# New instruction orders on TensorE, ScalarE and VectorE in a graph-attention stage, and its late weight preparation on GpSimd

## Chip, cores and metric

The kernel runs on one NeuronCore of one Trainium2 chip. The metric is the device time of one execution in microseconds (us); lower is better. It is measured three times for the kernel before, and once more under the profiler.

## What is computed

Two layers run one after the other on x (16 graphs, 512 nodes, 128 features). The first, the graph layer, is the stage that the change touches:

```
def _gat(h, adj, W, a, out_features):
    Wh = h @ W
    e = leaky_relu(Wh @ a[:F] + swapaxes(Wh @ a[F:], 1, 2))
    att = softmax(where(adj > 0, e, NEG), axis=1)
    return att @ Wh
h = _gat(_gat(x, adj, W1, a1), adj, W2, a2)
h = layernorm(x + h)
x = layernorm(h + relu(h @ w_ff1 + b_ff1) @ w_ff2 + b_ff2)
```

The second layer is a relational attention with 8 heads: softmax(q k^T / 4), then a sum over four relations r of (attention where adj == r) @ (x @ Wv[r] + bv[r]), a projection, a layernorm and a GELU feed-forward. Of it only one thing bears on the change: the kernel replaces Wv[r] and bv[r], r = 1 to 3, by their differences to Wv[0] and bv[0], and writes the biases as three bf16 parts that add up to the float32 value. This is prepared once, during the graph layer.

## The kernel before

`graph_layer` holds the stage. All of a graph's work fits the core at once, so the loop runs over graphs, 16 of them, as a software pipeline with a depth of four. In step t (the function `step`, one for each engine) graph t begins: its features are transposed and multiplied with the weights, its adjacency codes are made and transposed. Graph t-1 is in the first attention round, graph t-2 in the second round and the first layernorm, graph t-3 in the feed-forward and the second layernorm. Steps 0 to 3 are written out, steps 4 to 14 are a hardware loop (`eng.Fori`) of eleven turns, step 15 is written out again, and a `tail` with an order of its own drains the pipeline and starts the second layer. Nothing schedules this: each engine runs its instructions in the order in which `step` writes them, and semaphores (`wait_ge`, `then_inc`) tie the engines together.

Names on which the text rests, with the lines of this kernel:

- VectorE, `scores(k, b, ...)`: k = 1 is the second round (of graph t-2), k = 0 the first (of graph t-1). For each of four chunks of 128 rows it makes `leak` (L863: row[k] in PSUM and low[k] in SBUF, into att[k]) and `mask` (L870: att[k] and no_edge, both in SBUF, summed, with a running minimum). `edges` (L1027) makes no_edge from the codes of graph t-1. `invert` (L897) takes the reciprocals of the softmax sums, `scale_rows` (L904, four instructions) scales the rows of the first round, `see` (L943) gathers the codes seen so far, `add_h` (L1033) and `add_x` (L1040) are residual sums, `norm_stats` (L914, L921), `norm_shift` (L935) and `norm_finish` (L928) belong to the layernorms.
- ScalarE: `lower(k, b)` (L822) makes low[k] for `leak`; `exps` (L841) are the exponentials, one for each chunk; `hidden` (L835) the relus of the feed-forward; `centre` (L829), `rstds` (L847, L854), `keep_hw` (L809), `keep_x` (L815); L701 copies the transposed features x_t; L716 and L718 take the products with the weights out of PSUM.
- TensorE: `spread_row` (L555) makes row[k], `round_two` (L583) and `round_one` (L593) are the products with the attention, `turn_...` are transposes, `feed_up` (L567) and `feed_down` (L573) the feed-forward.
- GpSimd (Pool): `scale_hw` (L1064) makes hw_n for round_two as soon as `invert(1)` is done; `encode` (L467, four instructions) makes the next graph's codes, held back in this kernel by codes_seen, the semaphore of `see`. Its adjacency comes by a 1 MB transfer of the queue of SyncE.
- `Preparation.vector_late` (L161 to L192), fourteen instructions at the end of VectorE's step 1: the differences (L177, L178) and the split of the biases (L182 to L192), each waiting for the one before. It borrows memory of tiles that are not in use yet.

A turn of the loop ends on VectorE and begins like this, where `leak` of the second round waits for low[1]:

```
dve.wait_ge(row_ready[k], b + 1)
dve.wait_ge(low_ready[k], b + 1)
```

## Time and profile before

| what | us |
|---|---|
| median of 3 runs (lowest, highest) | 1195.62 (1195.38, 1196.02) |
| the profiled execution's own time | 1195.46 |
| its span, from first to last instruction | 1193.6 |
| one turn of the loop in the graph layer | 22.37 |
| busy in one such turn: TensorE, VectorE, ScalarE, GpSimd | 19.70, 18.96, 16.78, 5.49 |

The span leaves out 1.9 us around the instructions. Busy times come from the view that sums a stretch; a turn of the loop is taken from VectorE's first `leak` to the same one a turn later. In the timeline each row gives the start and the duration in us, the engine, the line, the operation, what it writes and reads, how many instructions are merged, and in brackets how long the engine had been idle and what ended that.

### The profile page before, as it was taken

The numbers are of one execution on the slowest core, as the hardware profiler recorded it, in microseconds if no ns is written. First come the engines' busy times: TensorE is split into PE (matmuls) and PEld (weight loads), VectorE is DVE, ScalarE is ACT, GpSimd is POOL, SyncE is SP. The second block draws the span as 40 slices with busy tenths as digits, with TensorE's granted clock in tenths as the row PEclk, the third lists the DMA queues.
The fourth block names the chain that finished last, engine by engine and source line by source line (L and its number), as shares of the span: only waits on it lengthen the run. The fifth ranks groups of instructions, "written<-read, shape, count | busy, mean of one in ns | idle before, by whom it ended". The sixth has DMA issues, their size and how long they took to land. (4 is left out here: it accounts for less than half of the span.)

```text
span 1193.6 us, 21838 instructions
## 1 busy us (share of the span) xinstructions
PE 1070.8 (90%) x6087; PEld 514.0 (43%) x6087; DVE 936.6 (78%) x2324; ACT 735.6 (62%) x1341; POOL 604.2 (51%) x513
## 2 busy tenths in 40 slices
PE   4588888888888869999999999999999999879996
PEld 3465666666664423333333333333333333234442
DVE  2878888888888757888888888889888887437777
ACT  3467778778777446666656666666656665544442
POOL 3231231231211157888888887888788887900000
PEclk9799999999999979999999999999999999989998
DMA  5313112112104133133322333143313320000000
GB/s 164 108 54 106 53 53 105 53 53 105 53 10 121 40 94 110 39 109 103 98 65 81 110 93 86 56 114 102 97 38 108 102 76 1 1 0 36 35 35 35
DMA packets 49546, 86.54 MB, mean 73 GB/s; under 512 B 8919, under 2 KB 35927, under 8 KB 44378
## 3 DMA queue, kind: packets, MB, share of 16 engines
q1 hardware_dynamic: 46586, 85.59, 23.4%
q10 hardware_dynamic: 2912, 0.40, 0.2%
q8 instruction: 20, 0.33, 0.1%
q14 instruction: 28, 0.23, 0.1%
HBM read 52.12 MB, written 29.36 MB: 68 GB/s over the span
## 5 line engine op out<-in xcount | busy, mean ns | idle before, releaser
L1493 DVE TENSOR_REDUCE top<-b_peak 128x1 f32<-128x512 f32 x488 | 320.4, 685 | 75.4 <-PE b_peak L1245 73.9
L1367 ACT ACTIVATE b_prob<-b_score 128x1024 f32<-128x1024 f32 x256 | 257.8, 1025 | 156.9 <-PE b_score L1260 111.5
L1630 POOL TENSOR_TENSOR b_picked<-b_prob,mask 128x512 f32<-128x512 f32 x192 | 233.8, 1238 | 61.6 <-ACT b_prob L1367 48.4
L1630 POOL TENSOR_TENSOR b_picked<-b_prob,b_mask 128x512 f32<-128x512 f32 x192 | 235.3, 1248 | 48.9 <-ACT b_prob L1367 38.3
L1064 POOL TENSOR_TENSOR a_hw_n<-a_hw,a_inv 128x512 f32<-128x512 f32 x16 | 16.6, 1040 | 211.3 <-DVE a_inv L897 199.7
L467 POOL TENSOR_SCALAR a_code<-a_adj_in 128x512 bf16<-128x512 int32 x64 | 71.9, 1123 | 83.5 <-DVE a_seen L943 55.1
L1245 PE MATMUL b_peak<-b_k_stack,b_q_stack 96*128 96x512 bf16 x256 | 98.4, 384 | 6.9 <-DVE top L1493 6.5
L841 ACT ACTIVATE a_att<-a_att,a_least 128x512 f32<-128x512 f32 x128 | 90.8, 714 | 16.0 <-DVE a_least L870 16.0
L1245 PE MATMUL b_peak<-shared 96*128 96x512 bf16 x232 | 90.2, 390 | 10.4 <-issue 6.4
L870 DVE CUSTOM_DVE_ANT_0 a_att<-a_att,a_no_edge 128x512 f32<-128x512 f32 x128 | 94.6, 757 | 0.0
L1747 ACT ACTIVATE c_hid<-c_mid,bff 128x512 f32<-128x512 f32 x64 | 44.0, 687 | 62.5 <-PE c_mid L1725 62.5
L1260 PE MATMUL b_score<-shared 98*128 98x512 bf16 x256 | 77.5, 384 | 0.0
L1260 PE MATMUL b_score<-b_q_stack,b_k_stack 98*128 98x512 bf16 x256 | 76.2, 379 | 0.0
L573 PE MATMUL a_out<-a_hid,wff 128*128 128x512 f32 x128 | 59.5, 605 | 18.5 <-ACT a_hid L835 18.5
L583 PE MATMUL a_turn<-a_hw_n,a_att 128*128 128x128 f32 x512 | 63.2, 283 | 13.0 <-POOL a_hw_n L1064 13.0
L583 PEld LDWEIGHTS a_turn<-a_hw_n,a_att 128*128 128x128 f32 x512 | 60.8, 198 | 24.9 <-issue 24.9
L1286 PE MATMUL b_o_ps<-b_picked,b_dval 128*32 128x512 f32 x512 | 68.2, 604 | 2.8 <-POOL b_picked L1630 2.7
L1245 PEld LDWEIGHTS b_peak<-b_k_stack,b_q_stack 96*128 96x128 bf16 x256 | 24.6, 96 | 102.1 <-DVE top L1493 61.8
L1286 PE MATMUL b_o_ps<-b_prob,b_val 128*32 128x512 f32 x512 | 67.1, 595 | 1.5 <-ACT b_o_t L1378 0.5
L1286 PE MATMUL b_o_ps<-b_picked,dval 128*32 128x512 f32 x512 | 68.2, 605 | 0.0
L1286 PE MATMUL b_o_ps<-b_prob,val 128*32 128x512 f32 x512 | 67.0, 595 | 1.0 <-ACT b_o_t L1378 0.3
L593 PE MATMUL a_pair<-a_xw_n,a_att 128*128 128x130 f32 x512 | 62.8, 282 | 4.8 <-DVE a_xw_n L904 4.8
(216 smaller groups left out, 1970.4 us busy)
## 6 DMA issues: line engine op xcount, KB each, us to landing
a_adj_in<-in_adj SPq DMA_DIRECT2D x16, 1024.0 KB, 5.0
scratch<-shared SPq DMA_DIRECT2D x32, 384.0 KB, 3.0
shared<-scratch SPq DMA_DIRECT2D x16, 768.0 KB, 6.5
...
```

Source lines behind the costliest of these rows:

```text
L467: eng.tensor_scalar(code[:, c, :].rearrange("p (k q) -> p k q", k=C), adj_in[:, c, :].rearrange("p (q k) -> p k q", k=C), CODE_HI, CODE_LO ...
L573: mm = pe.matmul(out[:, :], w["wff2"][0][:, f, :], hid[:, f, :], start=(f == 0), stop=(f == FC - 1))
L583: mm = pe.matmul(turn[:, ic * D:(ic + 1) * D], att[1][:, jc, ic * P:(ic + 1) * P], hw_n[:, jc, :], start=(jc == 0), stop=(jc == C - 1))
L593: mm = pe.matmul(pair[:, ic // 2, at:at + D + 2], att[0][:, jc, ic * P:(ic + 1) * P], xw_n[:, jc, :], start=(jc == 0), stop=(jc == C - 1))
L841: act.activation(att[k][:, c, :], att[k][:, c, :], ACT.Exp, bias=least[k][:, c:c + 1], scale=-1.0, accum_out=total[k][:, c:c + 1]).then_in ...
L870: dve.tensor_tensor_reduce(att[k][:, c, :], att[k][:, c, :], no_edge[:, c, :], 1.0, HIGHEST, ALU.add, ALU.min, least[k][:, c:c + 1]).then_ ...
L1245: pe.matmul(peak[hh % 2][:, :], q_stack[par][0:K, h, c * P:(c + 1) * P], k_stack[par][0:K, h, :], start=True, stop=True).then_inc(sem("pea ...
L1260: mm = pe.matmul(score[u][:, k, :], k_stack[par][:, h, c * P:(c + 1) * P], q_stack[par][:, h, :], start=True, stop=True)
L1286: mm = pe.matmul(o_ps[32 * hh:32 * hh + 32, :], v[:, c, GH * g + hh, :], src[:, hh, :], start=(c == 0 and rel is None), stop=(c == C - 1 a ...
L1367: act.activation(prob[s % 2][:, 2 * u:2 * u + 2, :], score[u][:, :, :], ACT.Exp, scale=float(DH) ** -0.5).then_inc(sem("exp_ready"), 1)
L1493: dve.tensor_reduce(top[g][:, hh, c:c + 1], peak[hh % 2][:, :], AX.X, ALU.max, negate=True).then_inc(sem("peak_read"), 1)
L1630: pool.tensor_tensor(picked[(NR * s + rel) % 2][:, hh, :], prob[s % 2][:, hh, :], m, ALU.mult).then_inc(sem("picked_pool"), 1)
```

## The change

- ScalarE's order in a step: x_t is copied ahead of `lower(1)`; `lower(0)` of a graph moves from the following step into the graph's own step; the exponentials of the second round alternate with the relus; those of the first round come ahead of the copies out of the weights' products; `keep_hw` comes after `rstds(0)`.
- TensorE's order: x is transposed ahead of `spread_row(1)`; the first product of `feed_down` comes ahead of the last of `feed_up`, and each product of `feed_down` waits for its own relu; `spread_row(0)` comes ahead of `round_one`.
- VectorE's order: the first two `leak` of the first round come ahead of `edges`, and `invert(1)` follows `edges` at once; `see` comes ahead of `invert(0)`; `add_x` comes ahead of `norm_shift`.
- GpSimd: `encode` waits for `scale_rows` and no longer for `see`; the late preparation is made here, in three shares at the end of steps 1, 2 and 3, in memory of its own.

How VectorE's loop turn now stands, first from the last `mask` of the second round (L870 before, L858 now; two rows each) to the first `mask` of the first round. Before:

```order
L870 ISA a_att,a_least<-a_att,a_no_edge 128x512
L870 ISA a_least 128x1
L1026 REGISTER_ALU
L1027 ISA
L1027 TENSOR_SCALAR a_no_edge<-codes 128x2048
L863 SCALAR_TENSOR_TENSOR a_att<-a_row,a_s_own,a_low 128x512 x2
L868 REGISTER_ALU
L870 ISA a_att,a_least<-a_att,a_no_edge 128x512
```

And of the change:

```order
L858 ISA a_att,a_least<-a_att,a_no_edge 128x512
L858 ISA a_least 128x1
L871 REGISTER_ALU
L851 SCALAR_TENSOR_TENSOR a_att<-a_row,a_s_own,a_low 128x512 x2
L1019 ISA
L1019 TENSOR_SCALAR a_no_edge<-codes 128x2048
L885 RECIPROCAL a_inv<-a_total 128x4
L856 REGISTER_ALU
L858 ISA a_att,a_least<-a_att,a_no_edge 128x512
```

The two `leak` moved ahead of `edges` (L1027, now L1019), and `invert` (L885) now stands right behind `edges`; before it stood behind the second `mask`.

The same engine later in the turn, from the last `scale_rows` (L904, now L892) to the statistics of the first layernorm. Before:

```order
L904 TENSOR_SCALAR a_xw_n<-shared,a_inv 128x130
L943 TENSOR_TENSOR a_seen<-a_seen,codes 128x512
L914 BN_STATS a_stats<-a_mid 128x6 x4
L918 ISA
L921 BN_AGGR a_mv<-a_stats 128x2 x4
L935 SCALAR_TENSOR_TENSOR a_shift<-a_mv,a_rstd 128x4
L1038 REGISTER_ALU
L1040 ISA
L1040 TENSOR_TENSOR a_y<-a_turn,xs 128x512
L914 BN_STATS a_stats<-a_y 128x6 x4
```

And of the change:

```order
L892 TENSOR_SCALAR a_xw_n<-shared,a_inv 128x130
L902 BN_STATS a_stats<-a_mid 128x6 x4
L906 ISA
L909 BN_AGGR a_mv<-a_stats 128x2 x4
L1030 REGISTER_ALU
L1032 ISA
L1032 TENSOR_TENSOR a_y<-a_turn,xs 128x512
L923 SCALAR_TENSOR_TENSOR a_shift<-a_mv,a_rstd 128x4
L902 BN_STATS a_stats<-a_y 128x6 x4
```

`see` (L943) is gone from this place (it now stands four operations earlier), and `add_x` (L1040, now L1032) changed places with `norm_shift` (L935, now L923).

ScalarE where a turn ends and the next step begins (the rows behind the branch are the written-out step 15, in the loop's order), from `keep_hw` (L809) on. Before:

```order
L809 COPY a_hw<-a_pair 128x520
L847 ACTIVATE a_lnv<-a_mv,eps 128x4
L854 ACTIVATE a_rstd<-a_lnv 128x4
L738 REGISTER_ALU
L739 ISA
L739 COPY a_s_own<-shared 128x4
L815 ISA
L815 ACTIVATE xs<-a_mid,columns 128x512
L457 REGISTER_ALU
L457 COMPARE_AND_BRANCH
L822 ACTIVATE a_low<-a_row 128x512
L701 COPY a_x_t<-a_turn 128x512
```

And of the change, from `rstds(0)` on:

```order
L835 ACTIVATE a_lnv<-a_mv,eps 128x4
L842 ACTIVATE a_rstd<-a_lnv 128x4
L797 COPY a_hw<-a_pair 128x520
L803 ISA
L803 ACTIVATE xs<-a_mid,columns 128x512
L453 REGISTER_ALU
L453 COMPARE_AND_BRANCH
L696 COPY a_x_t<-a_turn 128x512
L810 ACTIVATE a_low<-a_row 128x512
```

`keep_hw` (now L797) stands behind `rstds(0)` (L835, L842), and the copy of x_t (L701, now L696) ahead of `lower(1)` (L822, now L810).

The core of the diff:

```diff
--- before.py
+++ after.py
@@ -63,7 +63,8 @@
         self.right = sb("right", [P, D + 4])
         NB = R * D
         self.rows = sb("rows", [3, NB])
-        self.rest, self.acc, self.part, self.part2 = [at[0:3, 0:NB] for at in lent]
+        self.rest, self.acc, self.part = sb("rest", [3, NB]), sb("acc", [3, NB]), sb("part", [3, NB], BF16)
+        self.chain_length = 0
 
         self.loaded, self.late_loaded = sem("loaded"), sem("late_loaded")
         self.ident_made, self.consts_made = sem("ident_made"), sem("consts_made")
@@ -158,38 +159,35 @@
     def vector(self, dve):
         dve.memset(self.w["eps"][:, :], LN_EPS).then_inc(self.consts_made, 1)
 
-    def vector_late(self, dve):
+    def pool_late(self, pool, share):
+
 
         D, R, w = self.z.D, self.z.R, self.w
-        rows, rest, part, part2, acc = self.rows, self.rest, self.part, self.part2, self.acc
-        count = [0]
+        rows, rest, part, acc = self.rows, self.rest, self.part, self.acc
 
         def then(ins):
-
-            count[0] += 1
+            self.chain_length += 1
             ins.then_inc(self.chain, 1)
-            dve.wait_ge(self.chain, count[0])
-
...
+            pool.wait_ge(self.chain, self.chain_length)
+
+        def row(k):
+            return w["ident"][0:3, k:k + 1].to_broadcast([3, R * D])
+
+        if share == 0:
+            pool.wait_ge(self.late_loaded, 16 * len(self.late_loads))
+            for r in range(1, R):
+                then(pool.tensor_tensor(w["wv"][:, r, :], w["wv"][:, r, :], w["wv"][:, 0, :], ALU.subtract))
+                then(pool.tensor_tensor(rows[:, r * D:(r + 1) * D], rows[:, r * D:(r + 1) * D],
+                                        rows[:, 0:D], ALU.subtract))
+            then(pool.tensor_copy(part[:, :], rows[:, :]))
+            then(pool.tensor_tensor(acc[:, :], part[:, :], row(0), ALU.mult))
+        else:
+            then(pool.tensor_tensor(rows[:, :], rows[:, :], part[:, :], ALU.subtract))
+            then(pool.tensor_copy(part[:, :], rows[:, :]))
+            then(pool.tensor_tensor(rest[:, :], part[:, :], row(share), ALU.mult))
+            then(pool.tensor_tensor(acc[:, :], acc[:, :], rest[:, :], ALU.add))
+        if share == 2:
+            pool.tensor_copy(w["bias3"][0:3, :], acc[:, :]).then_inc(self.biases_split, 1)
 
 
 class FirstQueries:
@@ -567,9 +563,9 @@
                 pe.matmul(mid[f % 2][:, :], w["wff1"][0][:, f * P:(f + 1) * P], h_t[:, :],
                           start=True, stop=True).then_inc(mid_done, 1)
 
-            def feed_down(b, between=(0,) * 5):
-                pe.wait_ge(hid_ready, FC * b + FC)
-                for f in range(FC):
+            def feed_down(b, chunks=range(4), between=(0,) * 5):
+                for f in chunks:
+                    pe.wait_ge(hid_ready, FC * b + f + 1)
                     mm = pe.matmul(out[:, :], w["wff2"][0][:, f, :], hid[:, f, :], start=(f == 0), stop=(f == FC - 1))
                     if f == FC - 1:
                         mm.then_inc(ff_done, 1)
@@ -595,10 +591,10 @@
                 mm.then_inc(hw_done, 1)
 
             def step(t, begin, first, second, feed, more):
+                if begin:
+                    turn_x(t)
                 if second:
                     spread_row(1, t - 2)
-                if begin:
-                    turn_x(t)
                 if feed:
                     turn_h(t - 3)
                 if begin:
@@ -610,17 +606,18 @@
                     x_weights(t)
                 if feed:
                     feed_up(t - 3, 2)
+                    feed_down(t - 3, (0,))
                     feed_up(t - 3, 3)
-                    feed_down(t - 3)
+                    feed_down(t - 3, (1, 2, 3))
                 if second:
                     round_two(t - 2)
                 if feed:
                     turn_y(t - 3)
+                if begin:
+                    spread_row(0, t)
                 if first:
                     pe.wait_ge(xw_ready, t + 1)
                     round_one(t - 1)
-                if begin:
-                    spread_row(0, t)
                 if feed:
                     turn_n(t - 3)
 
@@ -693,57 +690,48 @@
             def step(t, begin, first, second, feed, more):
                 if isinstance(t, int) and t == 2:
                     prep.scalar_late(act)
-                if second:
-                    lower(1, t - 2)
                 if begin:
                     act.wait_ge(x_turned, t + 1)
                     act.wait_ge(xw_done, t)
                     act.copy(x_t[:, :], turn[:, :]).then_inc(x_t_ready, 1)
-                if first:
-                    lower(0, t - 1)
+                if second:
+                    lower(1, t - 2)
                 if feed:
                     keep_h(t - 3)
                 if begin:
                     act.wait_ge(code_turned, t + 1)
                     act.copy(codes[:, t, :, :], code_ps[:, :, :]).then_inc(codes_kept, 1)
-                if feed:
-                    hidden(t - 3, 0)
-                    hidden(t - 3, 1)
+                for f in range(FC):
+                    if feed:
+                        hidden(t - 3, f)
+                    if second:
+                        exps(1, t - 2, ((0,), (1,), (2, 3), ())[f])
+                if first:
+                    exps(0, t - 1, range(C))
                 if begin:
                     act.wait_ge(xw_done, t + 1)
                     both = pair[:, :, 0:2 * (D + 4)]
+                    act.copy(xw[:, t, :, :].rearrange("p (a c) d -> p a (c d)", a=2), both).then_inc(xw_ready, 1)
                     act.wait_ge(row_ready[0], t)
                     act.copy(s1_own[:, :, :].rearrange("p (a c) o -> p a c o", a=2),
                              both.rearrange("p a (c d) -> p a c d", c=2)[:, :, :, D + 3:D + 4]).then_inc(s1_ready, 1)
-                    act.copy(xw[:, t, :, :].rearrange("p (a c) d -> p a (c d)", a=2), both).then_inc(xw_ready, 1)
-                if feed:
-                    hidden(t - 3, 2)
-                if second:
-                    exps(1, t - 2, (0,))
-                if feed:
-                    hidden(t - 3, 3)
-                if second:
-                    exps(1, t - 2, (1, 2, 3))
-                if first:
-                    exps(0, t - 1, range(C))
-                if feed:
-                    rstds(1, t - 3)
-                    centre(t - 3)
-                if first:
-                    keep_hw(t - 1)
-                if second:
-                    rstds(0, t - 2)
-                if begin:
+                    lower(0, t)
                     act.wait_ge(xw_ready, t + 1)
                     act.wait_ge(leaked[0], C * t)
                     act.copy(s2_own[:, :], xw[:, t, :, D + 2]).then_inc(s2_ready, 1)
                 if feed:
+                    rstds(1, t - 3)
+                    centre(t - 3)
+                if second:
+                    rstds(0, t - 2)
+                if first:
+                    keep_hw(t - 1)
+                if feed:
                     keep_x(t - 3)
 
             def tail():
 
                 lower(1, B - 2)
-                lower(0, B - 1)
                 keep_h(B - 3)
                 act.wait_ge(scaled[0], B - 1)
                 first_qk.first_part(act, pair[:, 0, :], 0, 0)
@@ -882,13 +870,13 @@
                         dve.wait_ge(round2_done, b)
                     dve.wait_ge(exp_ready[k], C * b)
                     leak(k, b, 0, s2)
-                    if k == 0:
-                        dve.wait_ge(edge_ready, b + 1)
                 for c in chunks:
                     if c + 1 < C:
-                        if c == 2:
-                            between()
                         leak(k, b, c + 1, s2)
+                    if c == 0:
+                        between()
+                        if k == 0:
+                            dve.wait_ge(edge_ready, b + 1)
                     mask(k, b, c)
 
             def invert(k, b):
@@ -953,24 +941,28 @@
             def step(t, begin, first, second, feed, more):
                 if second:
                     scores(1, t - 2, hw[:, :, D], range(C))
+                def between():
+                    edges(t - 1)
+                    if second:
+                        invert(1, t - 2)
+
                 if first:
-                    edges(t - 1)
-                    scores(0, t - 1, s2_own, range(C), (lambda: invert(1, t - 2)) if second else (lambda: None))
+                    scores(0, t - 1, s2_own, range(C), between)
                 if feed:
                     add_h(t - 3)
                 if first:
+                    see(t - 1)
                     invert(0, t - 1)
                     scale_rows(t - 1)
-                    see(t - 1)
                 if feed:
                     norm_stats(1, t - 3)
+                if second:
+                    add_x(t - 2)
+                if feed:
                     norm_shift(t - 3)
                 if second:
-                    add_x(t - 2)
                     norm_stats(0, t - 2)
                     norm_finish(t - 2)
-                if isinstance(t, int) and t == 1:
-                    prep.vector_late(dve)
 
             def most(start, stop):
                 for n in range(start, stop):
@@ -1052,8 +1044,10 @@
                     scale_hw(t - 2)
                 if more:
                     if first:
-                        pool.wait_ge(codes_seen, t)
+                        pool.wait_ge(scaled[0], t)
                     encode(pool, t + 1, range(C))
+                if isinstance(t, int) and 1 <= t <= 3:
+                    prep.pool_late(pool, t - 1)
                 if isinstance(t, int) and t == 3:
                     first_qk.pads(pool)
```

## Rows read from the trace of the kernel before

**Rows 1.** The page's first row: the span of the profiled execution.
```profile
span 1193.6 us, 21838 instructions
```

**Rows 2.** Busy us by engine (instructions), granted clock, DMA: one loop turn.
```profile
247.88:270.25 22.37, 19.70 (x128) 14.38 (x128) 18.96 (x56) 16.78 (x39) 5.49 (x5) 1.00 0.20 71
```

**Rows 3.** Timeline of VectorE, the same turn: start, duration, what, idle before.
```profile
246.56 1.41 DVE L863 SCALAR_TENSOR_TENSOR a_att<-a_row,a_hw,a_low 128x512 f32<-128x512 f32 x2 [0.57 <-ACT a_low L822]
...
256.93 1.29 DVE L870 CUSTOM_DVE_ANT_0 a_att<-a_att,a_no_edge 128x512 f32<-128x512 f32 x1
...
258.16 0.68 DVE L870 CUSTOM_DVE_ANT_0 a_att<-a_att,a_no_edge 128x512 f32<-128x512 f32 x1
...
258.77 0.74 DVE L1033 SCALAR_TENSOR_TENSOR a_y_t<-a_out,columns,a_h_t 128x512 f32<-128x512 f32 x1
259.82 0.18 DVE L897 RECIPROCAL a_inv<-a_total 128x4 f32<-128x4 f32 x1 [0.31 <-ACT a_att L841]
...
260.95 0.68 DVE L943 TENSOR_TENSOR a_seen<-a_seen,codes 128x512 int32<-128x512 int32 x1
262.11 0.89 DVE L914 BATCH_NORM_STATS2 a_stats<-a_mid 128x6 f32<-128x128 f32 x4 [0.48 <-PE a_mid L513]
264.13 0.16 DVE L935 SCALAR_TENSOR_TENSOR a_shift<-a_mv,a_rstd 128x4 f32<-128x4 f32 x1 [0.60 <-ACT a_rstd L854]
264.41 0.69 DVE L1040 TENSOR_TENSOR a_y<-a_turn,xs 128x512 f32<-128x512 f32 x1
265.13 0.87 DVE L914 BATCH_NORM_STATS2 a_stats<-a_y 128x6 f32<-128x128 f32 x4
```

**Rows 4.** Timelines of GpSimd, TensorE and ScalarE in the same turn.
```profile
256.64 1.04 POOL L1064 TENSOR_TENSOR a_hw_n<-a_hw,a_inv 128x512 f32<-128x512 f32 x1 [12.36 <-DVE a_inv L897]
261.94 4.68 POOL L467 TENSOR_SCALAR a_code<-a_adj_in 128x512 bf16<-128x512 int32 x4 [4.26 <-DVE a_seen L943]
...
257.82 3.81 PE L583 MATMUL a_turn<-a_hw_n,a_att 128*128 128x128 f32 x32 [0.28 <-POOL a_hw_n L1064]
...
255.09 0.71 ACT L841 ACTIVATE a_att<-a_att,a_least 128x512 f32<-128x512 f32 x1
...
265.71 0.60 ACT L809 COPY a_hw<-a_pair 128x520 f32<-128x520 f32 x1
...
266.89 0.20 ACT L854 ACTIVATE a_rstd<-a_lnv 128x4 f32<-128x4 f32 x1
...
267.92 0.59 ACT L822 ACTIVATE a_low<-a_row 128x512 f32<-128x512 f32 x1
268.39 0.58 ACT L701 COPY a_x_t<-a_turn 128x512 f32<-128x512 f32 x1
```

**Rows 5.** VectorE's timeline in step 3: the one long norm_shift.
```profile
84.37 1.02 DVE L935 SCALAR_TENSOR_TENSOR a_shift<-a_mv,a_rstd 128x4 f32<-128x4 f32 x1 [0.60 <-ACT a_rstd L854]
```

**Rows 6.** Timelines, steps 1 to 3; last, engines and clock of a stretch.
```profile
43.45 1.39 DVE L863 SCALAR_TENSOR_TENSOR a_att<-a_row,a_hw,a_low 128x512 f32<-128x512 f32 x2
...
36.25 5.50 POOL L467 TENSOR_SCALAR a_code<-a_adj_in 128x512 bf16<-128x512 int32 x4 [13.77 <-DMA a_adj_in<-in_adj]
...
54.58 6.12 PE L583 MATMUL a_turn<-a_hw_n,a_att 128*128 128x128 f32 x32 [8.38 <-POOL a_hw_n L1064]
60.54 3.75 PE L593 MATMUL a_pair<-a_xw_n,a_att 128*128 128x130 f32 x32
...
45.80:59.40 13.60, 5.22 (x25) 4.95 (x24) 11.35 (x28) 6.62 (x18) 1.95 (x2) 0.50 0.12 46
```

**Rows 7.** VectorE's first leak of steps 3, 4, 15 and of the tail.
```profile
66.53 1.41 DVE L863 SCALAR_TENSOR_TENSOR a_att<-a_row,a_hw,a_low 128x512 f32<-128x512 f32 x2
...
89.92 1.41 DVE L863 SCALAR_TENSOR_TENSOR a_att<-a_row,a_hw,a_low 128x512 f32<-128x512 f32 x2 [0.67 <-ACT a_low L822]
...
335.72 1.41 DVE L863 SCALAR_TENSOR_TENSOR a_att<-a_row,a_hw,a_low 128x512 f32<-128x512 f32 x2 [0.25 <-issue]
...
357.46 1.41 DVE L863 SCALAR_TENSOR_TENSOR a_att<-a_row,a_hw,a_low 128x512 f32<-128x512 f32 x2
```

26 lines of the change are left out of this document (3 added, 23 removed).

## Prediction

> **What bounds the kernel now.** I read the page first, then the busy time of one loop turn, then each engine's timeline over that turn, since the change lies in one stage and the averages of the page mix three. The span is 1193.6 us [rows 1]; the profiled execution's own time is 1195.5, which is 0.15 below the median of the runs, so I sum against 1195.5 and hand the result over unchanged. About 0.2%, 2.4 us, is what a measurement of this kernel can tell from no change.
>
> In a loop turn of 22.37 us TensorE is busy for 19.70 and VectorE for 18.96, at the full granted clock [rows 2]. No engine is the bound alone; a round through several is. Follow it in [rows 3, 4]: VectorE starts the turn with the first leak at 246.56; behind the second mask of the first round it makes invert(1), and hw_n follows on GpSimd at 256.64, 10.08 into the turn. TensorE has waited for it (0.28 in its bracket) and starts round_two at 257.82; then turn_y, and VectorE, idle for 0.48, starts the statistics at 262.11, at 15.55. From there the layernorm passes between VectorE and ScalarE (the bracket of norm_shift says 0.60 waited for rstd). ScalarE makes rstd(0) at 266.89, then two more operations, then low[1] at 267.92, and the next leak follows 1.01 after the start of low[1], at 268.93. What the reader should see is that VectorE stands idle in small pieces (0.48, 0.60, 0.31 for the last exponential) while it is on the path in the first 10 us, and that hw_n comes late only because VectorE gets to invert(1) late.
>
> **The change, by stretches of a turn.** I lay the new order out with the same durations.
>
> First stretch, leak to the statistics of the second layernorm: 15.55 before. Two masks and a leak that stood ahead of invert(1) now stand behind it: 2 x 0.61 (258.16 to 258.77 is one mask) and 0.66, and the pause in which edges waited for the last mask, 0.2 by my estimate. hw_n comes 7.97 into the turn in place of 10.08 [rows 3, 4]. Its exponentials must be ready too. The last of them ended 9.3 into the turn, at 255.9 [rows 4]; the two copies and the relu that stood ahead of it now stand behind, and lower(0) is gone from in front, about 1.9 together, so it ends near 7.4, just in time for invert(1) at 7.5. So round_two begins near 9.5 rather than 11.26 (257.82), and TensorE stops being the path here; what its own reorderings (feed_down in pieces, x first, spread_row(0) ahead of round_one) save lies beside VectorE's work, and I cost them at nothing. If VectorE were not the cover they would be worth the relu wait ahead of feed_down, about 1 us. What remains is VectorE's own work: 12.21 from the first leak to add_h (246.56 to 258.77), 0.66 for add_h (its 0.74 less the overlap with the next), 0.60 for see, which now fills the idle 0.31 ahead of invert(0), and 1.13 for invert(0) and scale_rows (259.82 to 260.95) [rows 3]. Sum 14.60: **0.95 saved**.
>
> In these 12.21 lies one stall. A mask took 1.29 in place of 0.68; it began at 256.93, while hw_n ran from 256.64 to 257.68, and ended 0.54 behind hw_n [rows 3, 4]. So a mask and hw_n do not run side by side. In the new order hw_n falls at 7.97, and the first mask of the first round at 7.7 to 7.9. I take it that the mask, being earlier, goes first, that hw_n then waits for it and the mask behind the next leak waits for hw_n: about 0.6 again. The bounds are 0.4 (the mask at 7.7, hw_n from 8.4 to 9.4 against a second mask due at 9.0) and 1.3 (the first mask waits for all of hw_n). The Trainium skill, page "SBUF — State Buffer", section "SBUF: two separate sides", says that GpSimd and a VectorE operation with two SBUF inputs take a shared port pair as an exclusive lock, the first for its whole instruction; by it the sum is the same if the mask is first, and 0.7 a turn worse if hw_n is.
>
> Second stretch, those statistics to the ones of the first layernorm: 3.02 before (262.11 to 265.13). From the first to norm_shift 2.02 passed, 0.60 of it the wait for rstd. Now add_x stands in that wait: 1.42, then add_x with its hand-over 0.72 (264.41 to 265.13), then norm_shift below 0.1: near 2.2, so 0.8 to 0.85 saved. But encode now starts behind scale_rows, 0.31 after its end, and norm_shift falls about 1.6 into encode, in the middle of the second of its four instructions (4.68 / 4 = 1.17 each). In step 3 one norm_shift took 1.02 where the rows of the loop have 0.16; encode was running there. In the loop it fell at 264.13, 2.19 into encode, where the second instruction ends [rows 3, 4, 5]. So I charge the rest of the second instruction, 0.7. Left: **0.15 saved**. The bounds are 0 and 0.7 for this charge.
>
> Third stretch, rstd(0) to the next leak: before, low[1] starts 1.03 after rstd(0), with the small copy s2 and keep_x between. Now s2 has gone ahead (0.2 less), and keep_hw (0.60) and the copy of x_t (0.58) stand between, about 0.5 each when packed [rows 4]. **0.8 lost**. Behind low[1] nothing changes.
>
> One turn: 22.37 - 0.95 - 0.15 + 0.80 = 22.07, 0.3 saved. Eleven turns run from the leak at 89.92 to the one at 335.72 [rows 7]: 3.3 saved.
>
> **The written-out steps.** Step 15 took 21.74 (335.72 to 357.46) [rows 7]. It makes no encode, so nothing blocks norm_shift: 0.95 + 0.85 - 0.8 = 1.0 saved. Step 3 took 23.39 (66.53 to 89.92), its norm_shift already blocked, and saves 1.0 likewise.
>
> Start. The fourteen late instructions hold VectorE at the end of step 1 until the first leak of step 2 starts, at 43.45 [rows 6]. They leave VectorE. The exponentials of graph 0 no longer wait for the weights' product of graph 1, so that leak can start near 39.5, 4 us earlier. Step 2 cannot follow at once: its codes need encode, which started at 36.25 when its 1 MB landed, and took 5.50 [rows 6]; undisturbed it takes 4.7 and ends at 40.9. From there, codes, exponentials and masks bring round_two of graph 0 to about 50.5 in place of 54.58. It still runs in the stretch of half clock (45.8 to 59.4, 0.50 granted, 1.2 GHz, behind TensorE's idle time) for 6.1 us; round_one, 3.75 at full clock, starts at 57.6, its first 1.8 us at half clock, and ends at about 62.1 in place of 64.3 [rows 6]. The leak of step 3 comes **2.1 earlier**. Bounds: 0.5, if the half clock lasts on through round_one, and 5, if it is not there.
>
> Shares on GpSimd. Seventeen instructions for fourteen, 8, 4 and 5 in a share. No row shows them on GpSimd; the nearest is hw_n, also two float32 inputs of 512 elements with a repeated operand, 1.04. I take a share for 4.5 to 5 us. GpSimd is free for that: 5.49 of 22.37 are busy. The next hw_n comes some 10 us behind encode's end, which hides them; without that cover each microsecond over 10 would go into round_two. What is not hidden is that two-input operations hold up masks, as above. A share behind encode reaches the first mask of the next step: 0.8 each for shares 1 and 2 (between 0 and 2 masks of 0.6), in all **1.6 lost**. The one of share 0 is in the 50.5 above.
>
> Tail. Its order is kept; feed_down starts as its relus come, at most 1 us on TensorE in front of the second-last round. I take **0.4 saved**. The second layer shifts with its start.
>
> Sum: 2.1 + 1.0 + 3.3 + 1.0 + 0.4 - 1.6 = 6.2 saved: 1195.5 - 6.2 = 1189.3.
>
> **Rivals.**
> - Norm_shift is free. For it: of the loop rows not one is long. Against: the long one in step 3 [rows 5]. Then 0.7 more for twelve steps: 8.4, 1181.
> - VectorE's stalls hide nothing and TensorE or the wait for low[1] keeps the turn at 22.4, because the wait chain at ScalarE's end (keep_hw now needs the end of round_one and rstd(0)) eats the gain. For it: ScalarE's tail is the one stretch that gets longer. Then only start and end are left: 1195.5 - 2.9 = 1192.6 to 1194, about no change.
> - Slower: hw_n takes its place first. The two meet within 0.2 us, once a step. From the point where invert(1)'s signal reaches GpSimd before edges' reaches the mask, the mask waits 1.3 in place of 0.6, so 0.7 in each of 14 steps, 9.8 lost: 1195.5 - 6.2 + 9.8 = 1199.1. For it: mask must wait for edges, whose row of the order stands only one short reciprocal ahead. Against: edges ends before the reciprocal does.
> - Also slower, little likely: shares over 10 us, with instructions three times those of hw_n. At 4 us each, 16, 16 and 20 delay round_two by some 20: near 1209.
>
> **How the numbers follow.** Forecast 0.40; norm_shift free 0.27; turn unchanged 0.17; hw_n first 0.12; slow shares 0.03; 0.01 rest. Faster takes the first two, the better end of the third: 0.75. Same 0.12. Slower 0.13, the fourth, the fifth and a spill of the third. The range reaches from norm_shift free with a start 3 us better, 1178, to just short of hw_n first, 1197.
>
> **What would show it.** Per turn, leak to leak: 22.1; 21.4 if norm_shift is free; 22.8 if hw_n is first. hw_n at 8 to 8.5 into the turn, round_two no longer with a wait of VectorE's stats behind it (no bracket at the first statistics). norm_shift near 0.85 in the loop, one mask near 1.0. keep_hw and x_t between rstd(0) and low[1], about 1.8 from rstd(0)'s start to low[1]'s. The first leak of step 3 near 64.4. It is wrong if round_two still waits for hw_n and VectorE for turn_y, if a share lasts over 10 us, or if the turn is not set by VectorE and ScalarE's end.

## The result and the profile after

The changed kernel takes 1180.65 us (median of 4 runs, 1179.79 to 1181.6) beside 1195.82 for the kernel before on the same chip (1195.38 to 1197.23): ratio 0.9871, 95% interval 0.9854 to 0.9888, so 15.2 us faster. The forecast was 1189.3, 6.2 us saved: the direction and the range held, the size did not. The spans of the two profiled executions differ by 13.9 (1193.6 [rows 1] and 1179.8 now, each rounded), and the accounts below are of those two. The page's first rows:

```profile
span 1179.8 us, 21861 instructions
PE 1078.0 (91%) x6087; PEld 519.0 (44%) x6087; DVE 929.5 (79%) x2310; ACT 735.2 (62%) x1341; POOL 625.9 (53%) x530
```

One loop turn on VectorE, from the first leak to the next; the columns are those of [rows 3], and the same operations stand at lower line numbers:

```profile
234.82 1.41 DVE L851 SCALAR_TENSOR_TENSOR a_att<-a_row,a_hw,a_low 128x512 f32<-128x512 f32 x2 [1.19 <-ACT a_low L810]
...
242.36 0.17 DVE L885 RECIPROCAL a_inv<-a_total 128x4 f32<-128x4 f32 x1
242.72 0.69 DVE L858 CUSTOM_DVE_ANT_0 a_att<-a_att,a_no_edge 128x512 f32<-128x512 f32 x1 [0.20 <-issue]
...
244.00 0.86 DVE L858 CUSTOM_DVE_ANT_0 a_att<-a_att,a_no_edge 128x512 f32<-128x512 f32 x1
...
246.67 0.74 DVE L1025 SCALAR_TENSOR_TENSOR a_y_t<-a_out,columns,a_h_t 128x512 f32<-128x512 f32 x1
...
249.04 0.89 DVE L902 BATCH_NORM_STATS2 a_stats<-a_mid 128x6 f32<-128x128 f32 x4
...
251.07 0.70 DVE L923 SCALAR_TENSOR_TENSOR a_shift<-a_mv,a_rstd 128x4 f32<-128x4 f32 x1
251.69 0.86 DVE L902 BATCH_NORM_STATS2 a_stats<-a_y 128x6 f32<-128x128 f32 x4
...
253.88 1.12 DVE L916 TENSOR_SCALAR a_y<-a_y,a_mv,a_rstd 128x128 f32<-128x128 f32 x4 [0.81 <-ACT a_rstd L842]
256.19 0.75 DVE L851 SCALAR_TENSOR_TENSOR a_att<-a_row,a_hw,a_low 128x512 f32<-128x512 f32 x1 [1.19 <-ACT a_low L810]
```

The other engines in that turn, as in [rows 4]:

```profile
242.78 1.53 POOL L1058 TENSOR_TENSOR a_hw_n<-a_hw,a_inv 128x512 f32<-128x512 f32 x1 [10.04 <-DVE a_inv L885]
249.44 4.71 POOL L463 TENSOR_SCALAR a_code<-a_adj_in 128x512 bf16<-128x512 int32 x4 [5.13 <-DVE a_xw_n L892]
...
240.98 2.74 PE L569 MATMUL a_out<-a_hid,wff 128*128 128x512 f32 x6
244.46 3.81 PE L579 MATMUL a_turn<-a_hw_n,a_att 128*128 128x128 f32 x32 [0.74 <-POOL a_hw_n L1058]
...
253.53 0.20 ACT L842 ACTIVATE a_rstd<-a_lnv 128x4 f32<-128x4 f32 x1
...
255.29 0.61 ACT L810 ACTIVATE a_low<-a_row 128x512 f32<-128x512 f32 x1
```

The order does what was laid out: hw_n comes 7.96 into the turn, the statistics follow VectorE's own work with no bracket, norm_shift is long (0.70), and low[1] starts 1.76 behind rstd(0). But the turn is **21.38**, not 22.07 (22.37 before). The stages, by the first leaks of the second round (before: [rows 6, 7]):

| stretch | before | after | difference | forecast |
|---|---|---|---|---|
| (to the leak of step 2) | 43.45 | 39.12 | -4.33 | -4, part of the next |
| to the leak of step 3 | 66.53 | 61.82 | -4.71 | -2.1 |
| step 3 | 23.39 | 22.61 | -0.78 | -1.0, and +0.8 of share 1 |
| 11 turns | 245.80 | 235.72 | -10.08 | -3.3, and +0.8 of share 2 |
| step 15 | 21.74 | 20.28 | -1.46 | -1.0 |
| step 16 (tail) | 23.41 | 24.52 | +1.11 | -0.4 |
| rest of the span | 812.8 | 814.8 | +2.0 | 0 |

The start of the trace, first VectorE then GpSimd:

```profile
57.77 4.13 DVE L916 TENSOR_SCALAR a_y<-a_y,a_mv,a_rstd 128x128 f32<-128x128 f32 x4 [0.72 <-ACT a_rstd L842]
61.82 1.40 DVE L851 SCALAR_TENSOR_TENSOR a_att<-a_row,a_hw,a_low 128x512 f32<-128x512 f32 x2
...
54.13 4.69 POOL L463 TENSOR_SCALAR a_code<-a_adj_in 128x512 bf16<-128x512 int32 x4 [4.72 <-DVE a_xw_n L892]
58.89 1.15 POOL L185 TENSOR_TENSOR a_rows<-a_rows,a_part 3x512 f32<-3x512 f32 x1
...
61.89 1.27 POOL L188 TENSOR_TENSOR a_acc<-a_acc,a_rest 3x512 f32<-3x512 f32 x1
```

Share 1 takes 4.3, near the 4.5 to 5 forecast; but it falls on norm_finish (L916) of the same step, and not on the first mask of the next, as the forecast had it: norm_finish takes 4.13 here and 3.35 in step 3, 1.12 in the loop. Its four instructions last 1.12, 1.31, 0.74 and 1.19 here, where each takes 0.34 in the loop before.

The late rest of the span is longer through the clock: these stretches of the windows view (before, then after; columns as in [rows 2]) ran at half clock in the second layer, which the change leaves alone.

```profile
1052.70:1059.50 6.80, 5.75 (x10) 2.75 (x11) 0.54 (x2) 4.77 (x8) 0.00 (x0) 0.50 0.00 1
```

```profile
1025.60:1046.10 20.50, 13.31 (x33) 5.71 (x26) 3.62 (x14) 7.23 (x13) 0.00 (x0) 0.50 0.00 0
```

In the profiles of the kernels below, the half clock behind the leak that ends step 16 adds up to between 20.5 and 41.0 us (the last 7 to 9 us of each span, at half clock in all of them, left out), and the rest of the span goes broadly with it, from 808.3 (split_alone, 20.5) to 814.8 (the change, 41.0; before, 812.8 and 27.3). So from here on a kernel is compared by its turn and its steps first, and by its total second.

### The profile page after: what moved, and what is told of

It reads as the page before. It is cut to its first block and busy times, and to the rows that moved or that the text cites. A ratio compares the mean times of both kernels' runs of the same rounds, so it can differ in the third digit from the quotient of the medians.

```text
span 1179.8 us, 21861 instructions
## 1 busy us (share of the span) xinstructions
PE 1078.0 (91%) x6087; PEld 519.0 (44%) x6087; DVE 929.5 (79%) x2310; ACT 735.2 (62%) x1341; POOL 625.9 (53%) x530
## 3 DMA queue, kind: packets, MB, share of 16 engines
q1 hardware_dynamic: 46586, 85.59, 23.6%
## 5 line engine op out<-in xcount | busy, mean ns | idle before, releaser
L1361 ACT ACTIVATE b_prob<-b_score 128x1024 f32<-128x1024 f32 x256 | 257.9, 1026 | 156.8 <-PE b_score L1254 111.5
L1058 POOL TENSOR_TENSOR a_hw_n<-a_hw,a_inv 128x512 f32<-128x512 f32 x16 | 23.2, 1448 | 163.1 <-DVE a_inv L885 161.7
L858 DVE CUSTOM_DVE_ANT_0 a_att<-a_att,a_no_edge 128x512 f32<-128x512 f32 x128 | 89.1, 714 | 2.5 <-issue 2.0
L563 PE MATMUL a_mid<-a_h_t,wff 128*128 128x512 f32 x128 | 64.9, 612 | 3.1 <-ACT a_h_t L790 3.0
```

The lines of the kernel that those rows point to most:

```text
L563: pe.matmul(mid[f % 2][:, :], w["wff1"][0][:, f * P:(f + 1) * P], h_t[:, :], start=True, stop=True).then_inc(mid_done, 1)
L858: dve.tensor_tensor_reduce(att[k][:, c, :], att[k][:, c, :], no_edge[:, c, :], 1.0, HIGHEST, ALU.add, ALU.min, least[k][:, c:c + 1]).then_ ...
L1361: act.activation(prob[s % 2][:, 2 * u:2 * u + 2, :], score[u][:, :, :], ACT.Exp, scale=float(DH) ** -0.5).then_inc(sem("exp_ready"), 1)
```

## The experiments

"Turn" is leak to leak in the loop. Undone parts are undone in the changed kernel, parts done alone are put into the kernel before.

### The preparation

**prep_on_dve**: the shares go back to VectorE, at the end of step 1.

```diff
+                if isinstance(t, int) and t == 1:
+                    dve.wait_ge(prep.ident_made, 5)
+                    for share in range(3):
+                        prep.pool_late(dve, share)
-                if isinstance(t, int) and 1 <= t <= 3:
-                    prep.pool_late(pool, t - 1)
```

> The changed kernel with the late preparation put back on VectorE, at the end of its step 1 (the same seventeen instructions). Theory A, the start is set by VectorE's and GpSimd's first two steps: in the changed kernel VectorE sits idle for 8.9 us ahead of the first leak of step 2, so that most of some 9 us of preparation fits there; leak of step 2 about 1 to 2 us later than 39.1, turns of the loop unchanged at 21.4, whole kernel 1 to 3 us slower than the changed one, near 1182.5. Theory B, the move of the preparation is what the start gained (4.7 us at the leak of step 3): about 5 us slower, near 1186.

Measured 1178.99 (1178.47 to 1179.7), ratio 0.9863 [0.9849, 0.9877]. The first leak of step 2 falls at 43.07, 3.95 later than in the change, but steps 2, 3 and 4 take 21.3, 21.1 and 21.4 in place of 22.7, 22.6 and 22.1. At the leak of step 5 (106.88 against 106.50) 0.4 is left of the head start. Moving the preparation gains nothing: both theories had this kernel slower than the change.

**only_prep**: the kernel before, with the preparation on GpSimd and nothing else.

```diff
-                if isinstance(t, int) and t == 1:
-                    prep.vector_late(dve)
...
+                if isinstance(t, int) and 1 <= t <= 3:
+                    prep.pool_late(pool, t - 1)
```

> The kernel before with nothing but the late preparation moved to GpSimd in three shares. Theory A, the orders carry the gain: turns stay at 22.37, the leak of step 2 comes 1.5 us earlier (low[1] was ready at 41.9, the leak started at 43.45), some of it lost again in held-up masks; between 1.5 us faster and 0.5 slower than before, near 1195. Theory B, the preparation carries the start's gain: 4 to 5 us faster, near 1191. A share lasts 4.5 to 5 us.

Measured 1198.36 (1196.58 to 1198.78), ratio 1.0022 [1.0008, 1.0036]: a little slower. The leak of step 2 comes 1.2 earlier, steps 2 to 4 take 25.2, 25.0 and 24.9, and the turn is 22.24. Step 3 on VectorE, then GpSimd:

```profile
89.03 4.46 DVE L924 TENSOR_SCALAR a_y<-a_y,a_mv,a_rstd 128x128 f32<-128x128 f32 x4 [0.72 <-ACT a_rstd L850]
92.46 1.40 DVE L859 SCALAR_TENSOR_TENSOR a_att<-a_row,a_hw,a_low 128x512 f32<-128x512 f32 x2
...
87.54 1.15 POOL L185 TENSOR_TENSOR a_rows<-a_rows,a_part 3x512 f32<-3x512 f32 x1
...
90.54 1.25 POOL L188 TENSOR_TENSOR a_acc<-a_acc,a_rest 3x512 f32<-3x512 f32 x1
```

norm_finish is four instructions without a pause between them, and all but the first are held up beside GpSimd's (0.40, 1.19, 1.41 and 1.70, each 0.34 when alone): 4.46 in place of 1.12, of which the last 1.0 is recorded beside the next leak.

**shares_after_norm**: shares 1 and 2 wait for norm_finish.

```diff
+                    if t >= 2:
+                        pool.wait_ge(norm_ready, t - 1)
                     prep.pool_late(pool, t - 1)
```

> The change, with shares 1 and 2 on GpSimd held until norm_finish of the same step is done. Theory A (what a share costs is that it overlaps norm_finish, 4.13 and 3.35 in place of 1.12): norm_finish is back at 1.1 to 1.2 in steps 2 and 3, those steps fall from 22.7 and 22.6 toward 21.4, less one mask that the end of the share may still hold up (0.6); 1.5 to 2.5 faster than the change, about 1178.5, and level with the preparation on VectorE. Theory B (the steps at the start are long for another reason, TensorE's start at half clock): they stay at 22.6, 1180.6.

Measured 1178.5 (1176.92 to 1179.72), ratio 0.9862 [0.9845, 0.9879]. norm_finish is back at 1.44 and 1.13:

```profile
59.07 1.44 DVE L916 TENSOR_SCALAR a_y<-a_y,a_mv,a_rstd 128x128 f32<-128x128 f32 x4 [0.72 <-ACT a_rstd L842]
62.29 1.41 DVE L851 SCALAR_TENSOR_TENSOR a_att<-a_row,a_hw,a_low 128x512 f32<-128x512 f32 x2 [1.78 <-PE a_row L551]
```

Step 3 falls from 22.6 to 21.5, as theory A says. Step 2 does not: 23.6. TensorE's half clock lasted from 40.9 to 54.6 here (42.6 to 52.8 in the change), and the leak waits 1.78 for TensorE's spread row. So the cost of a share is shown for step 3 (1.1); in step 2 it is mixed with the clock. The intervals of this kernel and of the change overlap.

### The orders in a turn

**encode_after_shift**: encode starts behind norm_shift.

```diff
-                    if first:
+                    if feed:
+                        pool.wait_ge(shift_ready, t - 2)
+                    elif first:
                         pool.wait_ge(scaled[0], t)
```

> The changed kernel with encode held until norm_shift is done (steps 3 and later). Theory P, GpSimd's encode and VectorE's small two-input norm_shift exclude one another: norm_shift 0.16 in place of 0.70, the turn 21.38 - 0.54 = 20.85, 6 us faster in all, near 1174.5; norm_finish, which then meets encode, may be held up, and beyond 0.6 of that the leak comes later by the rest, so the bound on the other side is a turn of 21.9. Theory Q, the 0.70 is a cost of norm_shift in its new place whatever GpSimd does: norm_shift stays at 0.70 and the time at 1180.6.

Measured 1199.12 (1197.45 to 1200.64), ratio 1.0031 [1.0016, 1.0046]. VectorE, GpSimd and TensorE at the end of a turn:

```profile
220.00 0.15 DVE L923 SCALAR_TENSOR_TENSOR a_shift<-a_mv,a_rstd 128x4 f32<-128x4 f32 x1
...
222.26 3.24 DVE L916 TENSOR_SCALAR a_y<-a_y,a_mv,a_rstd 128x128 f32<-128x128 f32 x4 [0.75 <-ACT a_rstd L842]
...
220.47 4.69 POOL L463 TENSOR_SCALAR a_code<-a_adj_in 128x512 bf16<-128x512 int32 x4 [7.22 <-DVE a_shift L923]
...
225.63 1.11 PE L502 MATMUL a_out<-ident,a_y 128*128 128x128 f32 x4 [2.19 <-DVE a_y L916]
```

norm_shift is free (0.15), so encode costs it 0.55 in the change. But now norm_finish lies under encode and takes 3.24, and TensorE waits 2.19 for it. Such a wait stands at the end of eleven steps, and 3.4 us of half clock follow in nine of them. The turns are 22.3 to 23.7, longer than either theory allowed. The early start of encode is what clears norm_finish: 0.55 is paid for 2.1.

**invert_behind_mask**: invert(1) behind the first mask in place of in front.

```diff
                    mask(k, b, c)
+                    if c == 0:
+                        behind()
...
                 def between():
                     edges(t - 1)
+
+                def behind():
                     if second:
                         invert(1, t - 2)
```

> The changed kernel with invert(1) behind the first mask of the first round. Theory P (a mask and hw_n exclude one another): hw_n starts about 0.9 later, the second mask waits for it and lasts about 1.3 in place of 0.86, the pause of 0.2 ahead of the first mask may go or stay; the turn 0.2 to 0.5 longer, 21.6 to 21.9, the whole 3 to 6 us slower. Theory R, the turn does not hang on that meeting: 21.4, no change, though round_two starts later. If TensorE were the bound, the later hw_n would show in full: a turn 0.9 longer, 11 us slower.

Measured 1186.38 (1184.22 to 1188.33), ratio 0.9924 [0.9908, 0.994], turn 21.90. Its VectorE and GpSimd:

```profile
247.53 1.29 DVE L858 CUSTOM_DVE_ANT_0 a_att<-a_att,a_no_edge 128x512 f32<-128x512 f32 x1
...
247.23 1.04 POOL L1062 TENSOR_TENSOR a_hw_n<-a_hw,a_inv 128x512 f32<-128x512 f32 x1 [11.04 <-DVE a_inv L887]
```

The mask meets the whole of hw_n and takes 1.29, as in [rows 3]. That is the 0.6 that the forecast charged. Beside the change's 0.86 it is 0.43 of the 0.52 by which the turn is longer; the rest is a longer pause (0.29) ahead of the first mask. In the change the mask and hw_n start within 0.1 of each other (242.72, 242.78), hw_n's reported 1.53 in place of 1.04 is read here as holding its wait for the mask, and it runs beside the leak, which keeps its 0.75; only 0.18 (0.86 less 0.68) reaches the next mask.

**dve_old_order**: VectorE's order of before in the change, the rest new.

```diff
-                    if c == 0:
-                        between()
...
+                        if c == 2:
+                            between()
...
                 if first:
-                    see(t - 1)
                     invert(0, t - 1)
                     scale_rows(t - 1)
+                    see(t - 1)
...
-                if second:
-                    add_x(t - 2)
                 if feed:
                     norm_shift(t - 3)
```

> The changed kernel with VectorE's step in its old order (edges first, invert(1) behind the second mask, see behind scale_rows, norm_shift ahead of add_x); all else as changed. Theory A, the turn is VectorE's work plus ScalarE's end, and VectorE's order carries the whole gain: a turn of 22.4 to 22.6 (about 15.0 + 3.02 + 1.84 + 1.76 + 0.90), up to 23.4 if norm_shift falls into an encode instruction; 11 us or more slower than the changed kernel, 1192 or more. Theory B, TensorE's and ScalarE's orders carry part of it: a turn between 21.6 and 22.2, 1184 to 1190.

Measured 1210.79 (1209.98 to 1214.88), ratio 1.0145 [1.012, 1.017]. Turns are 23.47 or 24.65, slower than before itself and than theory A allowed. On TensorE:

```profile
244.68 3.81 PE L579 MATMUL a_turn<-a_hw_n,a_att 128*128 128x128 f32 x32 [2.33 <-POOL a_hw_n L1052]
```

This wait of 2.33 to 2.35 stands in each of ten steps (5 to 14). In five of them half clock follows at once, and these are the turns of about 24.65; in the other five, the one shown among them, the clock stays full, and the turn is 23.47.

**dve_order_alone** is the opposite corner: the kernel before with VectorE's new order and encode's new gate.

```diff
+                    if c == 0:
+                        between()
...
+                    see(t - 1)
                     invert(0, t - 1)
                     scale_rows(t - 1)
-                    see(t - 1)
...
-                        pool.wait_ge(codes_seen, t)
+                        pool.wait_ge(scaled[0], t)
```

> The kernel before, with VectorE's new order and encode held until scale_rows; TensorE, ScalarE and the preparation as before. Theory A (the orders work only together): the exponentials of the second round end late for the earlier invert(1), so VectorE now waits there 1 to 2 and feed_down comes late for round_two; the turn is 22.4 to 24, 1196 to 1212. Theory B (VectorE's order is the whole of the gain): the turn is near 21.5, 1184 to 1187.

Measured 1201.49 (1198.55 to 1205.31), ratio 1.0061 [1.004, 1.0082], turn 22.98, at full clock in the loop. VectorE now waits for ScalarE's exponential, which ScalarE's old order puts behind two copies, a relu and lower(0):

```profile
258.92 0.18 DVE L897 RECIPROCAL a_inv<-a_total 128x4 f32<-128x4 f32 x1 [1.75 <-ACT a_att L841]
```

Each side alone is slower than before (22.98; 23.5 to 24.7), and both together take 21.38.

**feed_down_whole**: feed_down in one piece again, behind all relus.

```diff
-                    feed_down(t - 3, (0,))
                     feed_up(t - 3, 3)
-                    feed_down(t - 3, (1, 2, 3))
+                    pe.wait_ge(hid_ready, FC * (t - 3) + FC)
+                    feed_down(t - 3)
```

> The changed kernel with feed_down whole again, behind the last feed_up and waiting for the fourth relu. The prediction costed this reordering at nothing; by it the turn stays at 21.38, 1180.7. Against it stands the changed kernel's trace: the fourth relu ends at 242.4, so a whole feed_down would end near 246.15, 1.7 later than round_two starts now, and turn_y and VectorE's statistics would follow at about 250.4 in place of 249.04: by this theory a turn near 22.7, some 15 us slower, 1195.

Measured 1214.87 (1214.54 to 1215.26), ratio 1.0168 [1.0151, 1.0185], turn 23.90. TensorE, VectorE, then a stretch of the windows view:

```profile
240.69 5.40 PE L569 MATMUL a_out<-a_hid,wff 128*128 128x512 f32 x8 [2.13 <-ACT a_hid L823]
245.92 3.73 PE L579 MATMUL a_turn<-a_hw_n,a_att 128*128 128x128 f32 x32
...
246.21 0.75 DVE L1025 SCALAR_TENSOR_TENSOR a_y_t<-a_out,columns,a_h_t 128x512 f32<-128x512 f32 x1 [1.22 <-PE a_out L569]
...
250.13 0.89 DVE L902 BATCH_NORM_STATS2 a_stats<-a_mid 128x6 f32<-128x128 f32 x4 [1.45 <-PE a_mid L509]
...
241.60:245.00 3.40, 3.40 (x5) 1.33 (x4) 3.39 (x10) 2.22 (x5) 0.95 (x1) 0.50 0.00 0
```

TensorE stands idle for 2.13 and then has 1.2 GHz for 3.4 us, in every turn; feed_down takes 5.40 in place of 3.70 and holds round_two up. The piece that the forecast priced at nothing is worth 2.5 a turn, nearly twice what this experiment's second theory allowed (a turn near 22.7, 1195).

**split_alone**: only that split, in the kernel before.

```diff
-                pe.wait_ge(hid_ready, FC * b + FC)
-                for f in range(FC):
+                for f in chunks:
+                    pe.wait_ge(hid_ready, FC * b + f + 1)
...
+                    feed_down(t - 3, (0,))
                     feed_up(t - 3, 3)
-                    feed_down(t - 3)
+                    feed_down(t - 3, (1, 2, 3))
```

> The kernel before, with feed_down's first product put between the last two of feed_up and each product waiting for its own relu; nothing else. Theory A (the split pays only where hw_n is early; here round_two waits for hw_n whatever ends ahead of it): the turn stays at 22.2 to 22.4, 1194 to 1196. Theory B (the split is worth its 1.4 by itself): the turn is 21.5 or less, 1186 or less.

Measured 1212.73 (1210.57 to 1217.88), ratio 1.0162 [1.013, 1.0193]: neither theory. The split is harmful here:

```profile
241.72 2.74 PE L573 MATMUL a_out<-a_hid,wff 128*128 128x512 f32 x6
246.37 5.43 PE L583 MATMUL a_turn<-a_hw_n,a_att 128*128 128x128 f32 x32 [1.92 <-POOL a_hw_n L1065]
...
252.28 0.89 DVE L915 BATCH_NORM_STATS2 a_stats<-a_mid 128x6 f32<-128x128 f32 x4 [2.10 <-PE a_mid L513]
```

feed_down is done early, and round_two still waits for hw_n. In the kernel before, TensorE's idle time stood in two pieces, 0.28 for hw_n [rows 4] and 1.20 for the relu:

```profile
253.84 3.70 PE L573 MATMUL a_out<-a_hid,wff 128*128 128x512 f32 x8 [1.20 <-ACT a_hid L835]
```

Now it is one of 1.92, in every turn. In seven of the eleven half clock follows at once (246.6 to 250.0) and the turn is 24.68; in the other four it is 22.57. So work taken out from in front of a wait made the kernel 18 us slower, most of it through the clock: 2.1 in each of the seven turns, and 0.2 in every turn without it.

**act_end_old**: rstds(0) again behind keep_hw, lower(1) again ahead of the copy of x_t, spread_row(1) again ahead of turn_x.

```diff
+                if second:
+                    lower(1, t - 2)
                 if begin:
...
-                if second:
-                    rstds(0, t - 2)
                 if first:
                     keep_hw(t - 1)
+                if second:
+                    rstds(0, t - 2)
```

> The changed kernel with the end of ScalarE's turn as before: keep_hw ahead of rstds(0), lower(1) ahead of x_t, and TensorE's spread_row(1) ahead of turn_x. Theory A, that end is on the path with 0.73 lost there: low[1] starts about 0.36 earlier, but rstd(0) comes 0.4 later, since keep_hw waits for round_one, and norm_finish with it; a turn of 21.0 to 21.4, 0 to 4 us faster. Theory C, it is not on the path: no change within 0.1. If keep_hw's wait for round_one decides: a turn of 21.8, 4 us slower.

Measured 1181.62 (1180.4 to 1183.62), ratio 0.9886 [0.9869, 0.9904], turn 21.26. VectorE's brackets around that end:

```profile
259.15 1.11 DVE L916 TENSOR_SCALAR a_y<-a_y,a_mv,a_rstd 128x128 f32<-128x128 f32 x4 [1.30 <-ACT a_rstd L842]
260.51 1.41 DVE L851 SCALAR_TENSOR_TENSOR a_att<-a_row,a_hw,a_low 128x512 f32<-128x512 f32 x2 [0.24 <-ACT a_low L810]
```

The wait for low[1] falls from 1.19 to 0.24, and the one for rstd grows from 0.81 to 1.30, with 0.37 more for an exponential ahead of invert(1): of 0.95 only 0.12 is left, so that the turn lies in theory A's range and the total is no lower than the change's. In steps 2 to 4 it loses more (25.2, 24.8, 22.9).

### The tail, and all together

**tail_invert_early**: in the tail too, invert(1) behind the first mask.

```diff
-                scores(0, B - 1, s2_own, range(C // 2))
-                first_qk.remainder(dve, pair[:, 0, :], 0, 0)
+                scores(0, B - 1, s2_own, range(1))
                 invert(1, B - 2)
+                scores(0, B - 1, s2_own, range(1, C // 2))
+                first_qk.remainder(dve, pair[:, 0, :], 0, 0)
```

> The changed kernel with one line of the tail moved: invert(1) of graph 14 behind the first mask of graph 15's first round, in place of behind a remainder. In the changed kernel TensorE idles 3.0 us there for hw_n and round_two then takes 5.44, part of it at half clock, where it took 3.81 before. Theory A, this late hw_n is why the step behind the loop got 1.1 us longer: hw_n 1.3 earlier, the step 24.5 to about 23.2 or, with the half clock gone, 21.9; whole 1.3 to 2.6 faster, 1178.7. Theory B, something later in the tail holds it: no change.

Measured 1179.23 (1177.87 to 1184.55), ratio 0.9878 [0.9846, 0.991]; the step takes 25.14 in place of 24.52. In the change, and then here:

```profile
352.27 5.44 PE L579 MATMUL a_turn<-a_hw_n,a_att 128*128 128x128 f32 x32 [3.02 <-POOL a_hw_n L1058]
```

```profile
352.08 3.81 PE L579 MATMUL a_turn<-a_hw_n,a_att 128*128 128x128 f32 x32 [1.43 <-POOL a_hw_n L1059]
357.88 1.12 PE L509 MATMUL a_mid<-ident,a_y_t 128*128 128x128 f32 x4 [1.99 <-DVE a_y_t L1026]
359.28 4.79 PE L589 MATMUL a_pair<-a_xw_n,a_att 128*128 128x130 f32 x32 [0.28 <-DVE a_xw_n L892]
```

The wait for hw_n is halved and round_two has full clock, but TensorE then waits 1.99 for VectorE, and half clock follows there. VectorE is late because two of its masks are now held up where they took 0.68 in the change, one beside hw_n and one beside GpSimd's work for the second layer:

```profile
351.24 1.24 DVE L858 CUSTOM_DVE_ANT_0 a_att<-a_att,a_no_edge 128x512 f32<-128x512 f32 x1
...
354.39 1.20 DVE L858 CUSTOM_DVE_ANT_0 a_att<-a_att,a_no_edge 128x512 f32<-128x512 f32 x1
...
353.88 2.72 POOL L248 TENSOR_TENSOR shared<-shared 128x512 bf16<-128x512 f32 x2 [1.95 <-ACT shared L242]
```

VectorE is busy for 22.21 of this step in place of 21.14. No gain, and not the shorter step of theory A.

**combined**: shares_after_norm, act_end_old and tail_invert_early in one kernel, with the three edits above.

> The change with the three edits that each read a little faster: shares 1 and 2 held until norm_finish (1178.5), ScalarE's end and the first two of TensorE in the order of before (turn 21.26 in place of 21.38), and invert(1) behind the first mask in the tail (1179.2). Theory A (what the old end of ScalarE cost in steps 2 to 4 came through the shares, so holding them back removes that too): 2.1 + 1.3 + 1.4 off 1180.65, about 1176. Theory B (the three meet at the same places, or steps 2 to 4 are long with the old end whatever the shares do): 1178 to 1180, no better than shares_after_norm alone.

Measured 1180.54 (1177.42 to 1182.97), ratio 0.9859 [0.9832, 0.9887]: not to be told from the change, as theory B says. The turn is 21.27 and the profiled span 1176.1, but steps 2 and 16 take 23.5 and 25.3. All of step 16 has full clock here, though TensorE waits 2.00 in it, as long as in tail_invert_early; so half clock is not what keeps that step long once invert(1) is early. The lowest medians are those of shares_after_norm and prep_on_dve, 2.2 and 1.7 below the change; their intervals overlap its own, so none is shown to beat it.

## Why the prediction came out as it did

**The step that failed is the size of a turn**, and in it above all the second mask that was charged to hw_n: 22.07 forecast, 21.38 measured; 11 turns gave 10.1 in place of 3.3, which is 6.8 of the 7.7 by which the spans' difference of 13.9 exceeds the forecast's 6.2. (The other stretches nearly cancel: 2.6 more gained at the start and 0.5 in step 15, 1.5 and 2.0 lost in the tail and the rest; the shares are taken up below.) Its terms:

- *First stretch*, 14.60 forecast, 14.22 measured. The "about 0.6 again" for the mask was 0.18, plus a pause of 0.20 ahead of the first mask that was in the sum already. The forecast had the ingredients: its own lower bound, worked out from hw_n's position, was 0.4, and it charged a whole mask instead. A leak stands between the two masks, and hw_n can run beside it. invert_behind_mask shows the 0.6 that comes where the mask meets hw_n, and 0.52 of it in the turn.
- *Second stretch*, 2.87 forecast, 2.65 measured. norm_shift blocked: right, 0.55 for the 0.7 charged; and 0.61 in place of 0.72 passed from add_x to it. The Trainium skill, page "SBUF — State Buffer", section "SBUF: two separate sides", describes the shared port pair as an exclusive lock; norm_shift's 0.70 beside encode and 0.15 without it (encode_after_shift) agree.
- *Third stretch*, +0.80 forecast, +0.73 measured between rstd(0) and low[1]. Right, but act_end_old shows that the old order would give only 0.12 of it back: the alternatives end in other waits. From low[1] to the leak 0.11 less passed than before, which no run explains, and from the first layernorm's statistics to rstd(0) 0.08 more.

Together 0.7 a turn. Of these 0.7 no part is a mechanism that was missing; the missing one shows in the experiments. **"What its own reorderings ... save lies beside VectorE's work, and I cost them at nothing. If VectorE were not the cover they would be worth the relu wait ahead of feed_down, about 1 us"** was the wrong kind of argument: for the time of this change nothing was lost by it, since the layout of VectorE's work has TensorE out of the way, which the split makes true; but without the split the turn is 23.90, and with the split alone 22.57 to 24.68. The price of an idle stretch of TensorE is not its length alone: where it reached about 2, half clock followed in more than half of the turns.

**Start**: 4.71 gained to the leak of step 3, with share 1's cost in it, where 2.1 was forecast without one. The first leak at 39.12 was forecast (39.5). The forecast kept the half clock until 59.4; it ended at 52.8, and round_one (3.75 at 55.19) ran at full clock. The "bound 5, if it is not there" was the nearer end. That end moves: 52.8 to 56.5 in the kernels with the new orders, so part of the 4.7 may belong to the execution; each kernel was profiled once. And what is won there is lost again by step 4 (prep_on_dve): "4 us earlier" was right, and worth nothing at the end of step 4.

**Shares**: 4.3 to 6.2 each, forecast 4.5 to 5; "two-input operations hold up masks" was wrong in place: norm_finish is held up, by 3.0 and 2.2. Steps 2 to 4 together are 3.6 longer than with the preparation on VectorE, where 1.6 was charged.

**Tail**: -0.4 forecast, +1.1 measured. Before, feed_down waited 1.20 for its relus and round_two 1.35 for hw_n; now the pieces start as relus come, round_two waits 3.02 in one stretch, and half clock follows (353.2 to 356.6). Before, and then VectorE behind it in the change:

```profile
369.66 3.81 PE L583 MATMUL a_turn<-a_hw_n,a_att 128*128 128x128 f32 x32 [1.35 <-POOL a_hw_n L1064]
```

```profile
358.18 0.89 DVE L902 BATCH_NORM_STATS2 a_stats<-a_mid 128x6 f32<-128x128 f32 x4 [1.26 <-PE a_mid L509]
```

round_two starts 0.36 earlier in the step than before, but takes 5.44 in place of 3.81, and the statistics start 1.08 later: that is the 1.1, read from the two traces. tail_invert_early took the half clock from round_two and gained nothing, since VectorE's masks were then held up; so what a better order of the tail could win is not shown. **The rest** (+2.0) goes with the half clock at 1026 to 1046 in place of 1053 to 1060; what sets its length was not tried.

**The rivals.** Norm_shift free: not so (0.70). That the turn and the total are those named for this rival, 21.4 and 1181, is chance: other terms gave them. The lower end of the range, 1178, was built from it too, so that the range held owes something to luck. Turn unchanged at 22.4: not so; but with hw_n early and feed_down whole (feed_down_whole) it is 23.90, and with feed_down split and hw_n late (dve_old_order) 23.47 or 24.65, so it took both. hw_n first: not so; the mask starts 0.06 ahead. Where hw_n does stand ahead of a mask (invert_behind_mask) the turn is 0.52 longer, near the 0.7 forecast. Slow shares: none over 6.2. The chances of the last two rivals alone are 0.15, more than the 0.13 that the prediction gives to slower.

What stays open: ScalarE's alternation of relus and exponentials was not tried alone, nor VectorE's see and add_x; and why the clock falls behind one idle stretch of 1.92 or 2.33 and not behind the next.
